# The reciprocal roots of a turn's layer norm and group norm taken in one chain of steps

## The chip, the cores and the metric

The kernel runs on one NeuronCore of a Trainium2 chip. The metric is the device time of one execution in microseconds (us). Engines are named as in the profile: PE is TensorE (PEld its weight loads), DVE is VectorE, ACT is ScalarE, POOL is GpSimd, SP is SyncE.

## The reference

Input x has 16 samples of 256 vertices (or channels), each with 16x16 values. Two residual blocks follow each other, each fed by a group norm of 32 groups:

```python
x = x + _L0_conv_ref(_gn(x), ...)     # graph convolution with temporal and spatial attention
x = x + _L1_conv_ref(_gn(x), ...)     # mixture of 8 experts, the best 2 for each token

# end of _L0_conv_ref
y = jax.nn.relu(res + tc)
mu = jnp.mean(y, axis=-1, keepdims=True)
var = jnp.var(y, axis=-1, keepdims=True)
return (y - mu) / jnp.sqrt(var + 1e-05) * gamma + beta

def _gn(v, G=32, eps=1e-05):
    g = v.reshape(B_, G, C_ // G, H_, W_)
    m = jnp.mean(g, axis=(2, 3, 4), keepdims=True)
    s = jnp.var(g, axis=(2, 3, 4), keepdims=True)
    return ((g - m) / jnp.sqrt(s + eps)).reshape(v.shape)
```

The change is about the two places with `1 / sqrt(...)` in the middle of the kernel: the layer norm that ends the first block, and the group norm that begins the second.

## The kernel before, in words

The kernel has four stages: the temporal attention for groups of four samples, then the middle stage with one sample per turn (spatial attention, graph convolution, temporal convolution, layer norm, group norm, routing), then the 72 tiles of the experts, then the sum of both experts' rows with the residual.

The change lies in the middle stage. It is a software pipeline of 21 turns, i from -2 to 18. A turn works on six samples at once, each in another phase: `ahead2` is sample i+2 (product of the spatial attention), `ahead1` i+1 (softmax, features), `now` i (graph and temporal convolution), `back1` i-1 (layer norm), `back2` i-2 (group norm, tokens), `back3` i-3 (routing). Turns -2 to 3 and 14 to 18 are written out, turns 4 to 13 are five passes of a loop with two turns each. Every engine has its own `turn` that issues its share in a fixed order; an engine never overtakes, and semaphores `b_...` hold it until another engine's result is there.

On DVE some of the work is cut into generators. `weave(a, b, ...)` takes one step of each in rotation until all are through; `along=` names generators that get a step in each round, but are not waited for. So a chain of small steps, each waiting for the one before, is mixed with other work. DVE's turn is: `centre` (L1167 to L1173), `router(route_a)` with `statistics`, then `attention` (L1133 row maximum, L1136, then L1142, the reciprocal of the sums) along with the norm's generator and `choice` (`route_b`, the choice of experts, L1253 to L1274), then the rest of the norms with `matrices` (L1151 twice, L1126) and `choice`, and last `route_c` (L1282 to L1289, the slots of the tokens).

The steps that count below:

- `ln_b` (L1182) sums the squares, `ln_roots` takes 32 reciprocal roots, `ln_c` (L1202) scales the layer norm's values and lets POOL go on with `ln_out`: L892, L893, L895, three operations over 128x512 values. POOL's result is needed by DVE's `gn_stats` (L1207) in the next turn.
- `gn_moments` (L1219 to L1222) waits for PE's `gn_mean` (L516) by `b_g1`; PE's `gn_var` (L520) then gives `b_g2`; `gn_roots` takes two reciprocal roots and `gn_scale` (L1228, L1229) gives `b_nb`. That is what ACT's `normalise` (L769, then PE's tokens, L528) and PE's `prefix` (L549 to L553) wait for. DVE's L1282 waits for `prefix` by `b_pf`.
- L1142 waits for ACT's exponentials (L736). ACT's `scale` (L745) waits for L1142, and PE's `turn_softmax` (L474) for ACT.
- PE's order in a turn is logits L463, graph L492, mix L448, `gn_mean` L516, graph L492, `turn_softmax` L474, `gn_var` L520, graph L492, features L483, product L455, convolution L504 and L509, features L483, `prefix` L549 to L553, tokens L528 and L533, L541.

`reciprocal_root` is a guess from the bits and three Newton steps, with the first line 13 operations of DVE, each waiting for the one before:

Of the kernel before, what the change touches and what calls it, by code (L numbers as in the profile page):

```python
# [66 lines left out]
def done(b):  # L67

    return b + (1 + START)
# [48 lines left out]
def build(nc, x, consts, small, cheb, vst, bst, w13t, w2t, xrows, yrows, out):  # L118
    with ExitStack() as ctx:
# [3 lines left out]
        def sem(name):  # L123
            return ctx.enter_context(nc.semaphore(name))
# [123 lines left out]
        v_ln = sem("v_ln"); v_gn = sem("v_gn"); v_rt = sem("v_rt"); v_rt2 = sem("v_rt2"); v_rt3 = sem("v_rt3"); v_lq = sem("v_lq"); v_gq = sem("v_gq")  # L248
# [703 lines left out]
        def _(dve):  # L952
# [233 lines left out]
            def ln_roots(b, p):  # L1186
                dve.wait_ge(s["b_var"], done(b))
                step = Steps(dve, v_lq, b, 13)
                yield from step.then(V.tensor_scalar(vq[:, 0, LN], vq[:, 4, LN], 1.0 / T, EPS, ALU.mult, ALU.add))
                yield from reciprocal_root(step, vq[:, :, LN], vr[:, LN])  # L1190
                step.close()

            def gn_roots(b, p):
                dve.wait_ge(s["b_g2"], done(b))
                step = Steps(dve, v_gq, b, 13)
                yield from step.then(V.tensor_scalar(vq[:, 0, GN], bank[2][:, 0:C], EPS, None, ALU.add))
                yield from reciprocal_root(step, vq[:, :, GN], vr[:, GN])
                step.close()

            def ln_c(b, p):  # L1200
                yv = yvs[p]
                V.tensor_tensor(yv, yv, th(vr[:, LN]), ALU.mult).then_inc(s["b_dn"], 1)  # L1202
                yield
# [90 lines left out]
            def turn(i, q, ahead2, ahead1, now, back1, back2, back3):  # L1294
# [21 lines left out]
                def layer_norm():  # L1316
                    if back1:
                        yield from ln_b(i - 1, 1 - q)
                        yield from ln_roots(i - 1, 1 - q)
                        yield from ln_c(i - 1, 1 - q)  # L1320

                def group_norm():
                    if back2:
                        yield from gn_moments(i - 2, q, step)
                        yield from pause(2)
                        yield from gn_roots(i - 2, q)
                        yield from gn_scale(i - 2, q)
# [17 lines left out]
                variance = layer_norm()  # L1345
                weave(attention(), along=(variance, choice))
                weave(variance, group_norm(), matrices(), choice)
# [172 lines left out]
```

## Time and profile before

| | |
|---|---|
| median of 3 runs | 752.15 us (751.39 to 752.87) |
| span of the profiled execution | 748.2 us; its own time with what lies around the span is not listed |
| middle stage | from about 110 us to 430 us of the span |
| PE busy | 587.2 us (78%) |
| DVE busy | 429.4 us (57%), 1895 instructions |
| ACT, POOL busy | 251.6 us, 208.3 us |

The shares are means over four stages with different limits. In the loop of the middle stage (187 to 393 us of the span) PE and DVE are both busy for some nine tenths of the time, so that neither share alone says which one sets a turn's length. In the timeline the columns are start in us, duration in us, engine, line, operation, result <- operands, shapes, and xN where N neighbouring instructions are merged. A bracket at the end is the idle time of the engine just before, and what ended it.

### The profile page before, as it was taken

How to read it: one execution, taken by the hardware profiler on the slowest of the kernel's cores; microseconds unless marked ns; L12 is line 12 of the kernel's file. 1: busy time of each engine (PE TensorE's matmuls, PEld its weight loads, DVE VectorE, ACT ScalarE, POOL GpSimd, SP SyncE). 2: the span in 40 equal slices, each digit the busy share in tenths (PEclk: the TensorE clock that was granted, in tenths of full speed). 3: DMA queues.
4: the chain of work that ended last, by engine and by line, in shares of the span. 5: the costliest groups of instructions: out<-in, count | busy, mean ns of one | idle time of the engine just before them, and what ended most of it. 6: DMA issues, size and time to landing. Idle time of an engine off the chain costs nothing. (4 is left out here: it accounts for less than half of the span.)

```text
span 748.2 us, 13145 instructions
## 1 busy us (share of the span) xinstructions
PE 587.2 (78%) x2520; PEld 372.1 (50%) x2521; DVE 429.4 (57%) x1895; ACT 251.6 (34%) x626; POOL 208.3 (28%) x267
## 2 busy tenths in 40 slices
PE   0556669999999999999983328999999999999343
PEld 0333337766666666666661114555555555555222
DVE  6666423778989888888888633232332333232255
ACT  0312224454545444444422102232232322232232
POOL 1000000114333333333455321333333333333100
PEclk9866659999999999999995559999999999999655
DMA  8900000000000000000000141222222222221496
GB/s 262 401 8 0 0 1 1 0 1 30 30 29 28 28 28 28 28 28 28 28 30 29 57 107 57 71 78 71 77 73 80 70 77 76 75 80 54 136 306 231
DMA packets 36439, 52.82 MB, mean 71 GB/s; under 512 B 4669, under 2 KB 31552, under 8 KB 36160
## 3 DMA queue, kind: packets, MB, share of 16 engines
q1 hardware_dynamic: 24960, 30.99, 13.2%
q0 software_dynamic: 6528, 16.86, 6.5%
q10 hardware_dynamic: 4928, 4.72, 1.9%
q8 instruction: 8, 0.13, 0.1%
q14 instruction: 15, 0.12, 0.1%
HBM read 30.32 MB, written 23.27 MB: 72 GB/s over the span
## 5 line engine op out<-in xcount | busy, mean ns | idle before, releaser
L612 PE MATMUL bank<-w,xT 128*128 x288 | 139.2, 606 | 14.9 <-DVE xT L1406 12.4
L1395 DVE COPY xT<-bank 128x256 f32<-128x256 f32 x72 | 30.6, 425 | 165.6 <-PE bank L600 163.6
L935 POOL DMA_INDIRECT yrows<-xT,dest x72 | 70.4, 978 | 169.4 <-ACT xT L821 163.1
L492 PE MATMUL bank<-work 128*128 128x256 f32 x384 | 94.5, 389 | 0.0
L904 POOL DMA_INDIRECT xrows<-xtok,slot x64 | 64.1, 1001 | 82.2 <-DVEq L1292 67.5
L892 POOL TENSOR_TENSOR yg<-work,sml 128x512 f32<-128x512 f32 x16 | 18.0, 1125 | 223.7 <-DVE work L1202 223.7
L627 PE MATMUL bank<-w,xT 128*128 x288 | 76.4, 388 | 1.3 <-ACT xT L826 1.3
L612 PEld LDWEIGHTS bank<-w,xT 128*128 128x128 f32 x288 | 49.5, 192 | 54.8 <-issue 54.8
L492 PEld LDWEIGHTS bank<-work 128*128 128x128 f32 x384 | 71.3, 193 | 9.3 <-issue 0.8
L815 ACT ACTIVATE xT<-bank 128x256 f32<-128x256 f32 x72 | 27.7, 385 | 113.8 <-PE bank L612 113.8
L627 PEld LDWEIGHTS bank<-w,xT 128*128 128x128 f32 x288 | 49.0, 190 | 9.4 <-issue 5.7
L821 ACT COPY xT<-bank 128x256 f32 (+1 forms) x72 | 26.8, 372 | 71.1 <-PE bank L627 70.1
L600 PEld LDWEIGHTS bank<-cst,xT 128*128 128x128 f32 x144 | 17.7, 143 | 62.9 <-SPq L316 31.7
L483 PE MATMUL bank<-thetabd,xTb 128*128 128x384 f32 x128 | 46.6, 487 | 0.0
L600 PE MATMUL bank<-cst,xT 128*128 128x128 f32 x144 | 29.9, 290 | 15.3 <-SPq L316 15.3
L663 PE MATMUL bank<-cst,xT 128*128 128x128 f32 x64 | 17.8, 433 | 30.6 <-DVE xT L1428 30.6
L769 ACT ACTIVATE xn<-xs,gr 128x256 f32 (+1 forms) x32 | 17.5, 593 | 71.2 <-DVE gr L1229 71.2
L463 PE MATMUL bank<-sg,vs 128*128 128x256 f32 x128 | 33.4, 406 | 2.5 <-ACT sg L731 1.4
L1151 DVE TENSOR_TENSOR work<-bank,chebs 128x768 f32<-128x768 f32 x32 | 30.0, 946 | 5.1 <-PE bank L474 5.1
L1406 DVE TENSOR_TENSOR xT<-bank,xT 128x256 f32<-128x256 f32 x72 | 30.6, 425 | 2.0 <-ACT xT L815 2.0
L751 ACT COPY work<-bank 128x384 f32<-128x384 f32 x64 | 28.9, 473 | 7.2 <-PE bank L483 6.5
L528 PE MATMUL bank<-xn,sml 128*8 128x256 f32 x64 | 19.0, 426 | 14.4 <-ACT xn L769 14.4
(205 smaller groups left out, 1061.0 us busy)
## 6 DMA issues: line engine op xcount, KB each, us to landing
xT<-xrows SPq DMA_DIRECT2D x72, 129.0 KB
xT<-yrows SPq DMA_DIRECT2D x32, 256.0 KB, 4.0
xs<-x_in SPq DMA_DIRECT2D x4, 1024.0 KB, 6.4
w<-w13t_in SPq DMA_DIRECT2D x1, 4096.0 KB, 15.2
out<-xT ACTq DMA_DIRECT2D x16, 256.0 KB, 3.8
w<-w2t_in SPq DMA_DIRECT2D x1, 2048.0 KB, 19.4
yrows<-xT,dest POOLq DMA_INDIRECT x72, 2.4
xrows<-xtok,slot POOLq DMA_INDIRECT x64
```

The source lines that it names most:

```text
L463: last = mm(bank[1][:, c * N:(c + 1) * N], vs[:, j, c * P:(c + 1) * P], sg[:, p, j], start=(j == 0), stop=(j == C - 1))
L483: mm(bank[4 + h][:, 0:K * P], xTb[:, p, h, c * P:(c + 1) * P], thetabd[:].rearrange("p k t o -> p (k t o)"), start=True, stop=True).then_i ...
L492: last = mm(bank[6][:, h * N:(h + 1) * N], z[:, p, c, k, h], A[:, p, c, k], start=(c == 0 and k == 0), stop=(c == C - 1 and k == K - 1))
L600: last = nc.tensor.transpose(bank[q][:, c * P:(c + 1) * P], xt[:, q, c * P:(c + 1) * P], ident)
L612: last = mm(bank[2 + q][:, :], xc[:, q, c], w13[:, e, c].rearrange("p w n -> p (w n)"), start=(c == 0), stop=(c == C - 1))
L627: last = mm(bank[4 + q][:, 0:N], hT[:, q, f], w2[:, e, f], start=(f == 0), stop=(f == C - 1))
L751: nc.scalar.copy(z[:, p, c, :, h], bank[4 + h][:, 0:K * P].rearrange("p (k o) -> p k o", k=K)).then_inc(s["b_zc"], 1)
L904: pool.indirect_dma_start(xrows, bass.IndirectOffsetOnAxis(ap=slot[:, q, w, k:k + 1], axis=0), xtok[:, q, k], None).then_inc(sc_done[q], 16)
L935: pool.indirect_dma_start(yrows, bass.IndirectOffsetOnAxis(ap=dest[:, q], axis=0), yo[:, q], None, bounds_check=2 * TOKENS - 1, oob_is_err ...
L1151: ins = V.tensor_tensor(A[:, p, c], p3, chebs[:, c], ALU.mult)
L1395: V.tensor_copy(xc[:, q].rearrange("p c k -> p (c k)"), bank[q][:, 0:C * P]).then_inc(c_xc, 1)
L1406: V.tensor_tensor(hh[:, q].rearrange("p f k -> p (f k)"), bank[2 + q][:, C * P:2 * C * P], gl[:, q].rearrange("p f k -> p (f k)"), ALU.mul ...
```

## The change

`ln_roots` and `gn_roots` become one `roots`, which fills columns 0 to 31 of `vq` from the layer norm and columns 32 and 33 from the group norm and then takes one chain over 34 columns. It needs `b_var` and `b_g2` at its start. The generators `layer_norm` and `group_norm` become one `norms`, in the order `ln_b`, `gn_moments`, two pauses, `roots`, `ln_c`, `gn_scale`.

```diff
-            def ln_roots(b, p):
-                dve.wait_ge(s["b_var"], done(b))
-                step = Steps(dve, v_lq, b, 13)
-                yield from step.then(V.tensor_scalar(vq[:, 0, LN], vq[:, 4, LN], 1.0 / T, EPS, ALU.mult, ALU.add))
-                yield from reciprocal_root(step, vq[:, :, LN], vr[:, LN])
-                step.close()
-
-            def gn_roots(b, p):
-                dve.wait_ge(s["b_g2"], done(b))
-                step = Steps(dve, v_gq, b, 13)
-                yield from step.then(V.tensor_scalar(vq[:, 0, GN], bank[2][:, 0:C], EPS, None, ALU.add))
-                yield from reciprocal_root(step, vq[:, :, GN], vr[:, GN])
+            def roots(turn, of_ln, of_gn):
+
+                if of_ln:
+                    dve.wait_ge(s["b_var"], done(turn))
+                    ins = V.tensor_scalar(vq[:, 0, LN], vq[:, 4, LN], 1.0 / T, EPS, ALU.mult, ALU.add)
+                if of_gn:
+                    dve.wait_ge(s["b_g2"], done(turn - 1))
+                    ins = V.tensor_scalar(vq[:, 0, GN], bank[2][:, 0:C], EPS, None, ALU.add)
+                both = slice(0 if of_ln else C * 16, NV if of_gn else C * 16)
+                step = Steps(dve, v_rq, turn, 13)
+                yield from step.then(ins)
+                yield from reciprocal_root(step, vq[:, :, both], vr[:, both])
                 step.close()
...
-                def layer_norm():
+                def norms():
+
                     if back1:
                         yield from ln_b(i - 1, 1 - q)
-                        yield from ln_roots(i - 1, 1 - q)
-                        yield from ln_c(i - 1, 1 - q)
-
-                def group_norm():
                     if back2:
                         yield from gn_moments(i - 2, q, step)
                         yield from pause(2)
-                        yield from gn_roots(i - 2, q)
+                    if back1 or back2:
+                        yield from roots(i - 1, back1, back2)
+                    if back1:
+                        yield from ln_c(i - 1, 1 - q)
+                    if back2:
                         yield from gn_scale(i - 2, q)
...
-                variance = layer_norm()
-                weave(attention(), along=(variance, choice))
-                weave(variance, group_norm(), matrices(), choice)
+                both = norms()
+                weave(attention(), along=(both, choice))
+                weave(both, matrices(), choice)
```

The wait for both norms' inputs stands in new lines: L1189 before is L1190 now, L1196 is L1193. The other lines named here keep their numbers. PE, ACT, POOL and SP issue what they issued before, in the same order.

The first place is on DVE in turn 3 (every later turn up to 14 has the same order), from the last step of the row maximum, L1136, to the reciprocal L1142 of the softmax. Before:

```order
L1136 TENSOR_SCALAR nmx<-nmx 128x2 [waits v_mx]
L1189 TENSOR_SCALAR vq<-vq 128x32 [waits b_var]
L1254 RECIPROCAL r<-r 128x2 [waits v_rt2]
L992 TENSOR_SCALAR vq<-vq 128x32 [waits v_lq]
L1255 TENSOR_TENSOR rt<-rt,r 128x16 [waits v_rt2]
L993 TENSOR_SCALAR vr<-vq 128x32 [waits v_lq]
L1258 TENSOR_REDUCE r<-rt 128x2 [waits v_rt2]
L1142 RECIPROCAL es<-es 128x2 [waits b_exp]
```

The same place in the changed kernel, up to the first step that waits for `b_g2`:

```order
L1136 TENSOR_SCALAR nmx<-nmx 128x2 [waits v_mx]
L1219 COPY gd<-bank 128x2 [waits b_st,b_g1]
L1220 TENSOR_TENSOR gd<-mv,bank 128x2
L1254 RECIPROCAL r<-r 128x2 [waits v_rt2]
L1221 TENSOR_TENSOR gd<-gd 128x2 [waits v_gn]
L1255 TENSOR_TENSOR rt<-rt,r 128x16 [waits v_rt2]
L1222 TENSOR_TENSOR gd<-gd,mv 128x2 [waits v_gn]
L1258 TENSOR_REDUCE r<-rt 128x2 [waits v_rt2]
L1142 RECIPROCAL es<-es 128x2 [waits b_exp]
L1259 TENSOR_TENSOR rt<-rt,r 128x16 [waits v_rt2]
L1260 TENSOR_TENSOR rt<-rt,cst 128x16 [waits v_rt2]
L1193 TENSOR_SCALAR vq<-bank 128x2 [waits b_g2]
```

The group norm's moments moved ahead of L1142, the layer norm's first steps moved behind it, and nothing but two steps of `route_b` and L1190 (left to DVE between L1260 and L1193) stands between L1142 and the wait for `b_g2`.

The second place is the end of the same turn on DVE, from the last L1151 to the first steps of `route_c`. L1202 stands there now; before, it stood right ahead of the two rows L995 and L1267, some 20 rows earlier:

```order
L1151 TENSOR_TENSOR work<-bank,chebs 128x768
L1273 TENSOR_TENSOR wts<-r 128x2 [waits v_rt2]
L1274 TENSOR_TENSOR wts<-r 128x2
L1001 TENSOR_TENSOR vr<-vr,vq 128x34 [waits v_rq]
L1126 TENSOR_TENSOR sg<-bank,bs 128x512 [waits b_L,b_pr]
L1202 TENSOR_TENSOR work<-work,vr 128x512 [waits v_rq,v_rt2]
L1228 COPY gr<-vr 128x2 [waits b_xn]
L1229 SCALAR_TENSOR_TENSOR gr<-gd,vr 128x2
L1282 TENSOR_TENSOR rt<-bank,cnt 128x16 [waits b_pf]
L1283 TENSOR_TENSOR cnt<-cnt,bank 128x8 [waits v_rt3]
L1284 TENSOR_TENSOR rt<-rt,cst 128x16
L1285 TENSOR_TENSOR rt<-rt 128x16 [waits v_rt3]
```

Here before:

```order
L1151 TENSOR_TENSOR work<-bank,chebs 128x768
L1273 TENSOR_TENSOR wts<-r 128x2 [waits v_rt2]
L1274 TENSOR_TENSOR wts<-r 128x2
L996 SCALAR_TENSOR_TENSOR vq<-vq,vr 128x2 [waits v_gq]
L1126 TENSOR_TENSOR sg<-bank,bs 128x512 [waits b_L,b_pr]
L1003 SCALAR_TENSOR_TENSOR vr<-vq,vr 128x2 [waits v_gq,v_rt2]
L995 TENSOR_TENSOR vq<-vq,vr 128x2 [waits v_gq]
L996 SCALAR_TENSOR_TENSOR vq<-vq,vr 128x2 [waits v_gq]
L999 SCALAR_TENSOR_TENSOR vq<-vq,vr 128x2 [waits v_gq]
L1001 TENSOR_TENSOR vr<-vr,vq 128x2 [waits v_gq]
L1228 COPY gr<-vr 128x2 [waits b_xn,v_gq]
L1229 SCALAR_TENSOR_TENSOR gr<-gd,vr 128x2
```

The last five steps of the group norm's own chain are gone from behind L1126, and L1202, which lets POOL begin, came to stand between L1126 and L1228.

## Rows read from the trace of the kernel before

**Rows 1.** The head of the page.

```profile
span 748.2 us, 13145 instructions
```

**Rows 2.** Timeline of DVE: L1136 in turns 4 and 13, L1121 after a loop pass.

```profile
185.41 0.32 DVE L1136 TENSOR_SCALAR nmx<-nmx 128x2 f32<-128x2 f32 x1
...
216.72 0.21 DVE L1121 COPY ghb<-gh 128x96 f32 x1 [0.77 <-DVE slot L1289]
...
350.48 0.16 DVE L1136 TENSOR_SCALAR nmx<-nmx 128x2 f32<-128x2 f32 x1
```

**Rows 3.** Timeline of one turn of the loop, DVE and PE, to the next L1136.

```profile
222.33 0.16 DVE L1136 TENSOR_SCALAR nmx<-nmx 128x2 f32<-128x2 f32 x1
...
223.57 0.17 DVE L1142 RECIPROCAL es<-es 128x2 f32<-128x2 f32 x1 [0.47 <-ACT pe_ L736]
...
224.88 0.60 PE L474 MATMUL bank<-cst,pn 128*128 128x128 f32 x4
...
225.70 0.15 DVE L1196 TENSOR_SCALAR vq<-bank 128x2 f32<-128x2 f32 x1
...
226.52 0.69 DVE L1202 TENSOR_TENSOR work<-work,vr 128x512 f32<-128x512 f32 x1
...
229.58 0.94 DVE L1151 TENSOR_TENSOR work<-bank,chebs 128x768 f32<-128x768 f32 x1
...
231.19 0.68 DVE L1126 TENSOR_TENSOR sg<-bank,bs 128x512 f32<-128x512 f32 x1
231.26 1.45 PE L483 MATMUL bank<-thetabd,xTb 128*128 128x384 f32 x4
...
232.83 0.15 DVE L1229 SCALAR_TENSOR_TENSOR gr<-gd,vr 128x2 f32<-128x2 f32 x1
...
233.04 0.18 PE L549 MATMUL bank<-mb,tri 128*128 128x8 bf16 x1 [0.32 <-DVE gr L1229]
...
233.35 0.18 DVE L1282 TENSOR_TENSOR rt<-bank,cnt 128x16 f32<-128x16 f32 x1 [0.37 <-PE bank L553]
...
233.65 0.17 DVE L1284 TENSOR_TENSOR rt<-rt,cst 128x16 f32<-128x16 f32 x1
...
234.26 1.03 PE L528 MATMUL bank<-xn,sml 128*8 128x256 f32 x4 [0.95 <-ACT xn L769]
234.42 0.17 DVE L1289 CAST slot<-slotf 128x4 int32<-128x4 f32 x1
...
234.85 0.21 DVE L1121 COPY ghb<-gh 128x96 f32 x1 [0.26 <-DVE slot L1289]
...
240.28 0.16 DVE L1136 TENSOR_SCALAR nmx<-nmx 128x2 f32<-128x2 f32 x1
```

**Rows 4.** The same turn: POOL's three operations and DVE beside them.

```profile
227.30 1.12 POOL L892 TENSOR_TENSOR yg<-work,sml 128x512 f32<-128x512 f32 x1 [5.66 <-DVE work L1202]
227.32 1.12 DVE L996 SCALAR_TENSOR_TENSOR vq<-vq,vr 128x2 f32<-128x2 f32 x1
...
228.50 1.14 POOL L893 TENSOR_TENSOR yg<-yg,sml 128x512 f32<-128x512 f32 x1
...
229.83 1.27 POOL L895 TENSOR_TENSOR xs<-xs,yg 128x512 f32 x1 [0.19 <-POOL yg L893]
230.45 0.67 DVE L1273 TENSOR_TENSOR wts<-r 128x2 f32 x1
```

**Rows 5.** Timeline of PE in turn 3.

```profile
168.35 0.38 PE L516 MATMUL bank<-mv,cst 128*128 128x2 f32 x2
...
169.97 0.60 PE L474 MATMUL bank<-cst,pn 128*128 128x128 f32 x4
```

**Rows 6.** Timeline of DVE at the end of turns 15 and 16.

```profile
392.80 1.07 DVE L1228 COPY gr<-vr 128x2 f32<-128x2 f32 x1
...
401.84 0.16 DVE L1196 TENSOR_SCALAR vq<-bank 128x2 f32<-128x2 f32 x1
...
408.16 0.15 DVE L1229 SCALAR_TENSOR_TENSOR gr<-gd,vr 128x2 f32<-128x2 f32 x1
```

More of the change, by code:

```diff
@@ L247, in build @@
         s = {n: sem(n) for n in names}
-        v_ln = sem("v_ln"); v_gn = sem("v_gn"); v_rt = sem("v_rt"); v_rt2 = sem("v_rt2"); v_rt3 = sem("v_rt3"); v_lq = sem("v_lq"); v_gq = sem("v_gq")
+        v_ln = sem("v_ln"); v_gn = sem("v_gn"); v_rt = sem("v_rt"); v_rt2 = sem("v_rt2"); v_rt3 = sem("v_rt3"); v_rq = sem("v_rq")
         p_x1 = sem("p_x1"); v_mx = sem("v_mx")
```

## The prediction

> **What bounds the kernel now.** The page gives the profiled span, 748.2 us [rows 1]; the runs' median is 752.15, so 3.95 us lie around the span, and I carry a difference of spans over to the median. I then read the timeline of DVE for the length of a turn: L1136 comes at 185.41 in turn 4 and at 350.48 in turn 13, 165.07 us for nine turns, 18.34 each [rows 2]. The turn from 222.33 to 240.28 is one of the short ones, 17.95 [rows 3]; every second one is longer by the loop's branch (0.77 us idle ahead of L1121 in place of 0.26, and 5.61 in place of 5.43 from L1121 to L1136) [rows 2, 3].
>
> Which engine sets these lengths is read from the waits. PE stands still twice at a turn's end, 0.32 us ahead of L549 for DVE's L1229, and 0.95 ahead of L528 for ACT, which itself waited for L1229 [rows 3]. DVE in the same turn waits 0.47 us for ACT's exponentials and 0.37 for L549 to L553, and otherwise issues one step after the other. So DVE bounds the turn, and PE has about 1.3 us to spare. Part of DVE's time is not its own: L996, over two columns, took 1.12 us and ended with POOL's L892, which had started 0.02 us earlier; L1273 took 0.67 and ended with POOL's L895. L1229, also over two columns and with two operands from SBUF, takes 0.15 [rows 3]. In the tail a two-column copy, L1228, took 1.07 the same way [rows 4, 6]. What these three have in common is data read from SBUF on both engines.
>
> **The change, step by step.** I lay out a loop turn anew, with time 0 at the start of PE's L474 (224.88 in rows 3).
>
> Removed: 12 small instructions per full turn. While several generators take turns, one costs about 0.1 us (the eight rows from L1196 to L1202 take 0.82) [rows 3]; the last five of the group norm's chain are alone and wait for each other, 0.2 each, from L1126's end at 231.87 to L1228 just ahead of L1229. With the 1.0 us that L996 lost to POOL and the 0.5 of L1273, some 3.2 us of DVE's turn go. Two columns more per step are nothing beside that: L1202 takes 0.69 us for 512 columns [rows 3], which makes 0.003 for two.
>
> Moved, first: L1219 goes ahead of L1142, and waits for L516. In the loop PE is early there once DVE is later, see below, so L1142 still comes 1.24 after L1136, set by the exponentials. L474 follows 1.31 behind L1142 [rows 3]. No change here.
>
> Moved, second: the whole chain waits for `b_g2`. L520 stands behind L474 on PE, and L1196, which waited for it, came 0.82 after L474 began, so 2.13 after L1142 [rows 3]. That time was filled with layer norm steps before. Now DVE has L1259, L1260 and L1190, 0.3 us, and then stands still for about 1.7 us. L1193 is at 0.8. Behind it are all of `route_b`, both L1151, L1126, L1202 and L1229.
>
> From L1193: 20 rows in rotation up to the first L1151, 2.3 us; both L1151 with two rows between, 1.87; L1273, L1274, L1001, 0.2; L1126, 0.6; so L1202 is at 0.8 + 5.0 = 5.8, and L1229, 0.7 later, at 6.5. Before it was at 232.83 - 224.88 = 7.95. The chain's saving is thus 1.45 us, the stall already paid.
>
> Now the rest of the turn. PE ends the second L483 at 232.71, 7.83 after L474, and nothing before that depends on the moved steps, so `prefix` can't start sooner. L1282 comes 0.31 after L549's start: 8.15 where it was 8.47. Of the 1.45 us, 0.3 are left: **PE's own order takes the rest**, and DVE waits about 1.1 us for `b_pf`.
>
> Moved, third: L1202 from 1.64 to 5.8. POOL's L892 starts 0.78 behind it, at 6.55 (L1228 and L1229 are issued just ahead and slip by); L893 runs from 7.75 to 8.9, L895 from 9.1 to 10.35 [rows 4]. Before, all three were over at 6.2, ahead of `route_c`; now they lie upon it. L1284 reads two SBUF operands at 8.45 and is held to 8.9. L1285 and L1286 are issued 0.05 and 0.15 later, in the 0.19 us between L893 and L895. L1289, a cast from SBUF to SBUF, would start at 9.5 and is held to 10.38 if it behaves as the copy in rows 6 did. L1121 comes 0.26 behind, at 10.64. Before it was at 9.97. From there to the next L1136 and L474 nothing changes.
>
> So a short turn grows by 0.67, to 18.6. For a long one the same sum gives 10.38 + 0.77 + 5.61 + 2.55 = 19.3. Their mean is 18.95 against 18.34: **+0.6 us a turn, for ten turns +6**.
>
> The rule weighed against these rows: the Trainium skill, "SBUF — State Buffer", section "Who interferes with whom", says that `copy`, `cast` and `tensor_scalar` can all take the port pair that VectorE shares with GpSimd, that a VectorE instruction with two SBUF inputs contends with a GpSimd instruction that reads SBUF, and that the one issued first keeps the other out altogether. Rows 4 and 6 agree for two inputs and for a copy; no row shows a cast beside POOL. By the rule L1289 is held and the sum is +6 for the loop; by a reading of the rows that leaves casts free, it is the second rival below.
>
> Turns outside the loop. In turn 3 PE is the later one: L516 ends at 168.73, L1219 is held until then, L1142 comes seven small rows later at 169.4, and L474 at 170.7 where it was 169.97 [rows 5]. Turn 2, with no `route_c`, comes out within 0.3 of before by the same sum. With the held rows of `route_c`, which in unrolled turns meet a shorter gap on POOL (below), turn 3 costs +2. In turns 14 to 16 PE has less to do, there is no attention, and DVE's chain is bare. From L1196 to L1229 in turn 16 takes 6.32 us, with L996's kind of hold twice and a held copy [rows 6]. One chain of 12 steps at 0.22, L1202 and L1228 make 3.4: -2.9. Turn 15 has the same structure, but POOL's work falls on its `route_c`; I keep -1.0 for turns 14 and 15 together. Sum: +6 + 2 - 3.9 = **+4**. Time 752.15 + 4 = 756.
>
> **Unknown costs, from both sides.** A cast beside POOL: at least 0.17, its time alone [rows 3], at most until L895 ends, 0.9; I take the latter. L1286 against L895: free if issued in the gap, otherwise held until L895 ends, which puts L1289 behind it and costs 0.5 more a turn; I take free in the loop, held in the unrolled turns. The wait of L1219 in the loop: L516 ended at 223.64, 1.3 behind L1136; as L1121 now comes 0.67 later against the same PE order, and more against PE's own pace, between 0 and 0.3; I take 0, and up to 0.5 is hidden behind the exponentials.
>
> **The rivals.**
>
> A, *faster*: POOL doesn't hold up `route_c`, because L892 to L895 meet only instructions that are issued ahead of them. Then L1289 is at 9.2, L1121 at 9.65, a turn costs -0.3 to -0.4, the loop -4; with turn 3 at +0.6 and the tail's -4.5 that is -8, so 744. For it: rows 4 show instructions that slip by. Against it: L1284 and L1289 fall well inside L893 and L895. L895 ends 4.55 behind L1202's start and L1289 is due 3.7 behind it, so it decides when L1202 comes 0.9 earlier against L1282 than I have it, or when POOL is that much quicker.
>
> B, *no change*: the cast isn't held. Only L1121, a copy, is, until 10.4. A turn is then within 0.1 of what it was, turn 3 costs +1.5, the tail gives -3.9: -2, so 750. For it: nothing in the rows shows a cast held. Against it: the copy.
>
> C, *slower still*: L1286 is held in the loop as well. +1.1 a turn, +11 for the loop, +9 in all: 761. The margin is 0.05 us, so it is open.
>
> D, the group norm's result being earlier shortens the turn as a whole, since L549 and L528 stop waiting. PE's idle 1.3 us would go, ten times, 13 us with the tail 739 or less. Against it: L474 then waits for L1142 instead, and the loop L474, `b_g2`, chain, `b_pf`, L1136, L1142, L474 is closed over both engines. It would need L1142 not to move with `route_c`.
>
> **How the numbers follow.** My forecast has 0.48, C 0.17, B 0.15, A 0.12, D 0.03, and 0.05 for slower yet. A measurement of this kernel tells about 0.2%, 1.5 us, from no change. Slower holds mine, C and the rest, less the low edge of mine: 0.64. B is split between faster and same; with the low edge of mine, same has 0.15 and faster 0.21. The range goes from 748.5, between B and A, to 762, the upper side of C. My forecast's own range is 753 to 759.
>
> **What would show it.** After the change L1142 stands as before 1.25 behind L1136. L1193 shows a wait of 1.5 us or more for L520 in the loop. PE's L549 no longer waits for L1229, L474 waits for ACT by 1 us or so instead. L1282 waits about 1 us for L553. L996 and L1273 have lost their long cases; L1284 and L1289 take 0.5 and 1 us. L1136 repeats at 18.9 us. The tail from L1193 to L1229 in turn 16 takes 3.4 us. I am wrong if L1289 shows 0.17 throughout, if L1286 shows over 1 us in the loop, or if L1219 waits so long that L1142 comes later than 1.3 behind L1136.

## The result and the profile after

The changed kernel took 762.12 us, median of 4 runs (760.19 to 763.9), against 751.77 (750.63 to 752.87) for the kernel before: 10.35 us more, ratio 1.0141 with a 95% interval of 1.0109 to 1.0173. The forecast was 756.0 with a range of 748.5 to 762.0. The sign was right, the size was not: the median lies just above the range.

The head and the first two rows of the page after:

```profile
span 760.5 us, 12883 instructions
...
PE 592.6 (78%) x2520; PEld 374.7 (49%) x2521; DVE 412.6 (54%) x1715; ACT 252.0 (33%) x626; POOL 208.2 (27%) x267
```

DVE is 17 us less busy than the 429.4 of before and has 180 instructions fewer, and the kernel is slower. What was removed is gone; the time went into waits.

One short turn of the loop after, DVE, PE and POOL, in the columns of [rows 3]. Time 0 of the prediction is 272.07:

```profile
269.58 0.16 DVE L1136 TENSOR_SCALAR nmx<-nmx 128x2 f32<-128x2 f32 x1
...
270.83 0.17 DVE L1142 RECIPROCAL es<-es 128x2 f32<-128x2 f32 x1 [0.43 <-ACT pe_ L736]
...
272.07 0.66 PE L474 MATMUL bank<-cst,pn 128*128 128x128 f32 x4 [1.92 <-ACT pn L745]
...
272.88 0.16 DVE L1193 TENSOR_SCALAR vq<-bank 128x2 f32<-128x2 f32 x1 [1.48 <-PE bank L520]
...
278.13 0.68 DVE L1202 TENSOR_TENSOR work<-work,vr 128x512 f32<-128x512 f32 x1
...
278.80 0.16 DVE L1229 SCALAR_TENSOR_TENSOR gr<-gd,vr 128x2 f32<-128x2 f32 x1
278.90 1.12 POOL L892 TENSOR_TENSOR yg<-work,sml 128x512 f32<-128x512 f32 x1 [9.99 <-DVE work L1202]
...
280.10 0.17 DVE L1282 TENSOR_TENSOR rt<-bank,cnt 128x16 f32<-128x16 f32 x1 [1.14 <-PE bank L553]
280.10 1.12 POOL L893 TENSOR_TENSOR yg<-yg,sml 128x512 f32<-128x512 f32 x1
...
280.38 0.87 DVE L1284 TENSOR_TENSOR rt<-rt,cst 128x16 f32<-128x16 f32 x1
...
281.38 0.17 DVE L1286 TENSOR_TENSOR rt<-rt 128x16 f32<-128x16 f32 x1
281.41 1.27 POOL L895 TENSOR_TENSOR xs<-xs,yg 128x512 f32 x1 [0.19 <-POOL yg L893]
...
281.86 0.85 DVE L1289 CAST slot<-slotf 128x4 int32<-128x4 f32 x1
283.08 0.21 DVE L1121 COPY ghb<-gh 128x96 f32 x1 [0.37 <-DVE slot L1289]
...
288.45 0.16 DVE L1136 TENSOR_SCALAR nmx<-nmx 128x2 f32<-128x2 f32 x1
```

The reader is to see three things. L1202, which stood 1.64 behind L474 [rows 3], now stands 6.06 behind it, and POOL's three operations with it. L1284 takes 0.87 and ends with L893; L1289 takes 0.85 and ends with L895, where both took 0.17 before. L1286, issued 0.03 us ahead of L895, takes 0.17. And L1229, 6.73 behind L474 where it was at 7.95, hardly helps: L1282 comes 8.03 behind L474 after a wait of 1.14, where it was at 8.47, and L1121 11.01 behind it, where it was at 9.97.

The windows of the same trace, one row for each stretch (its bounds and length, busy time and count of PE, PEld, DVE, ACT and POOL, then the granted clock of TensorE, whose 1.00 is the level of 2.4 GHz and whose 0.5 is that of 1.2, then the share and the GB/s of the DMA engines):

```profile
229.94:250.18 20.24, 18.32 (x87) 12.86 (x86) 14.71 (x72) 8.75 (x21) 7.40 (x7) 0.92 0.06 23
...
234.00:238.00 4.00, 4.00 (x10) 2.38 (x9) 3.95 (x23) 1.46 (x3) 0.00 (x0) 0.62 0.00 0
...
189.87:385.41 195.54, 174.88 (x867) 125.05 (x866) 149.26 (x691) 86.91 (x210) 74.36 (x71) 0.97 0.08 27
```

The short turn above took 18.87. The one from 229.94 took 20.24, and over four of its microseconds the mean clock was 0.62, so TensorE was at the lower level for most of them. Over the same ten turns the kernel before had 183.16 us and a clock of 1.00. What PE did ahead of the fall:

```profile
232.42 0.66 PE L474 MATMUL bank<-cst,pn 128*128 128x128 f32 x4 [1.92 <-ACT pn L745]
...
233.05 2.33 PE L492 MATMUL bank<-work 128*128 128x256 f32 x6
...
235.18 2.40 PE L483 MATMUL bank<-thetabd,xTb 128*128 128x384 f32 x4
```

It stood still for 1.92 us. Then six matmuls of L492 took 2.33 us, where they take 1.54 in other turns, and four of L483 2.40 instead of 1.45. Such turns are three of ten, 20.63, 20.24 and 20.22 us long; the other two short ones are 18.87 and 18.89, the long ones 19.39 to 19.44 (the last, with no branch behind it, 19.07). In the three turns PE is late with `prefix` (L1282 comes 9.7 behind L474 after a wait of 2.04), and L1285, two operands from SBUF, is the step that is held by L895 (1.24 in this one); L1284 and L1289 take 0.17.

The accounts of the two profiled executions (760.5 - 748.2 = +12.3):

| part of the span | before | after | difference |
|---|---|---|---|
| to the first L1136 (no changed instruction) | 109.92 | 112.55 | +2.6 |
| turns -1 to 2 | 56.23 | 55.89 | -0.3 |
| turn 3 | 19.26 | 21.43 | +2.2 |
| ten turns of the loop | 183.16 | 195.54 | +12.4 |
| turn 14 to the last L1289 | 61.12 | 58.21 | -2.9 |
| after it | 318.51 | 316.88 | -1.6 |

The first and the last row hold no changed instruction. The first stage of the other kernels, which is the same code, took 110.0 to 112.1 in their profiles, so its +2.6 is mostly scatter. The changed stage alone accounts for +11.3.

The tail, turn 16, beside [rows 6]:

```profile
418.20 0.16 DVE L1193 TENSOR_SCALAR vq<-bank 128x2 f32<-128x2 f32 x1
...
422.00 0.15 DVE L1229 SCALAR_TENSOR_TENSOR gr<-gd,vr 128x2 f32<-128x2 f32 x1
...
423.37 1.10 DVE L1286 TENSOR_TENSOR rt<-rt 128x16 f32<-128x16 f32 x1
...
424.79 1.02 DVE L1289 CAST slot<-slotf 128x4 int32<-128x4 f32 x1
```

From L1193 to L1229 it is 3.80 us, where it was 6.32 from L1196 on. Here both L1286 and L1289 are held.

### The profile page after: what moved, and what is told of

It reads as the page before. It is cut to its first block, busy times and chain, and to the rows that moved or that the text cites. A ratio compares the mean times of both kernels' runs of the same rounds, so it can differ in the third digit from the quotient of the medians.

```text
span 760.5 us, 12883 instructions
## 1 busy us (share of the span) xinstructions
PE 592.6 (78%) x2520; PEld 374.7 (49%) x2521; DVE 412.6 (54%) x1715; ACT 252.0 (33%) x626; POOL 208.2 (27%) x267
## 4 chain that ended last, share of the span: by engine, by line
PE 52%; DVE 21%; issue 12%; DMA 6%; ACT 5%; POOL 1%; SPq 1%; DVEq 1%; POOLq 0%; ACTq 0%
PE bank L612 14%; PE bank L627 7%; PE bank L483 6%; PE bank L492 5%; DMA xT<-yrows 4%; PE bank L382 3%; PE bank L455 2%; PE bank L600 2%; PE bank L504 2%; PE bank L509 2%; DVE work L1167 2%; PE bank L463 1%; PE bank L474 1%; ACT pe_ L736 1%; DVE work L1173 1%
## 5 line engine op out<-in xcount | busy, mean ns | idle before, releaser
L492 PE MATMUL bank<-work 128*128 128x256 f32 x384 | 96.3, 395 | 0.0
L892 POOL TENSOR_TENSOR yg<-work,sml 128x512 f32<-128x512 f32 x16 | 18.0, 1125 | 281.7 <-DVE work L1202 281.7
L492 PEld LDWEIGHTS bank<-work 128*128 128x128 f32 x384 | 72.0, 195 | 9.6 <-issue 0.8
L483 PE MATMUL bank<-thetabd,xTb 128*128 128x384 f32 x128 | 48.4, 502 | 0.0
L769 ACT ACTIVATE xn<-xs,gr 128x256 f32 (+1 forms) x32 | 17.5, 593 | 48.9 <-DVE gr L1229 48.9
L1151 DVE TENSOR_TENSOR work<-bank,chebs 128x768 f32<-128x768 f32 x32 | 30.2, 953 | 5.1 <-PE bank L474 5.1
L483 PEld LDWEIGHTS bank<-thetabd,xTb 128*128 128x128 f32 x128 | 24.5, 200 | 10.6 <-issue 1.5
```

The source lines that it names most:

```text
L483: mm(bank[4 + h][:, 0:K * P], xTb[:, p, h, c * P:(c + 1) * P], thetabd[:].rearrange("p k t o -> p (k t o)"), start=True, stop=True).then_i ...
L492: last = mm(bank[6][:, h * N:(h + 1) * N], z[:, p, c, k, h], A[:, p, c, k], start=(c == 0 and k == 0), stop=(c == C - 1 and k == K - 1))
L1151: ins = V.tensor_tensor(A[:, p, c], p3, chebs[:, c], ALU.mult)
```

## The experiments

All were timed beside the kernel before, which had a median of 750.41 beside experiments 1 to 4, 750.28 beside 5 to 8, 749.76 beside 9 to 11 and 750.8 beside 12. Ratios are to that median, with a 95% interval; where a median is set against one of another comparison, a difference of 1 or 2 us says little. The questions came in this order: is it the place of POOL's work; what do the clock's falls cost; do the moved moments or PE's order cost anything; which arrangement would use what the merged chain gives.

**1. The kernel before with only L1202 moved behind the group norm's chain.**

```diff
                 def layer_norm():
                     if back1:
                         yield from ln_b(i - 1, 1 - q)
                         yield from ln_roots(i - 1, 1 - q)
-                        yield from ln_c(i - 1, 1 - q)
+                        if not back2:
+                            yield from ln_c(i - 1, 1 - q)
...
                         yield from gn_roots(i - 2, q)
+                        if back1:
+                            yield from ln_c(i - 1, 1 - q)
                         yield from gn_scale(i - 2, q)
```

> The kernel before with two separate chains, and one thing moved: where a turn has both norms, ln_c (L1202), which lets POOL begin, is issued after the group norm's chain, just ahead of gn_scale, as in the changed kernel. Theory P (place of POOL's work): the merged chain itself is worth next to nothing, since it ends where the group norm's own chain would end; what costs is that L892 to L895 now lie on route_c, hold L1284 and L1289, and that PE waits long for L745 ahead of L474. So this kernel is slower than before by 6 to 11 us, about as the changed one (10 us). Rival Q (the stall at b_g2 and the moments ahead of L1142 cost it): this kernel has neither, DVE does layer norm steps while it waits, so it is within 2 us of before.

763.77 us, ratio 1.0177 (1.0132 to 1.0223): as slow as the changed kernel, though two chains run as before and nothing waits for `b_g2` any earlier. Its timeline, of a long turn in which L474 began at 289.91, shows the same holds:

```profile
296.73 0.15 DVE L1229 SCALAR_TENSOR_TENSOR gr<-gd,vr 128x2 f32<-128x2 f32 x1
296.82 1.12 POOL L892 TENSOR_TENSOR yg<-work,sml 128x512 f32<-128x512 f32 x1 [9.34 <-DVE work L1202]
...
298.23 0.95 DVE L1284 TENSOR_TENSOR rt<-rt,cst 128x16 f32<-128x16 f32 x1
...
299.79 0.84 DVE L1289 CAST slot<-slotf 128x4 int32<-128x4 f32 x1
```

The place of L1202, and of POOL's work with it, is enough for the whole loss. The stall for `b_g2` isn't needed to explain any of it. PE's waits at L474 are 1.4 to 2.1 us here too, and three of the ten turns, at 20.6 to 20.7 us, have a fall of the clock.

The experiment also tells what the merged chain gives by itself. L1229 comes 6.82 behind L474 in this turn and 6.93 in a short one without a fall, against 6.73 in the changed kernel: nearly all of the 1.22 us by which it came earlier there are had with two chains, by moving L1202 alone.

**2. Two idle matmuls ahead of the wait for ACT on PE** (they write a bank that nobody needs then; line numbers rise by 2).

```diff
             def turn_softmax(b, p):
-                pe.wait_ge(s["b_pn"], done(b))
                 pe.wait_ge(s["b_A"], done(b - 1))
...
+                    for _ in range(2):
+                        mm(bank[3][:, 0:N], vs[:, 0, 0:P], bs[:, 0], start=True, stop=True)
+                pe.wait_ge(s["b_pn"], done(b))
                 for m in range(C):
```

> The changed kernel with two extra 128x256 matmuls per turn on PE (into bank 3, which the transposes overwrite right after) between the graph product and turn_softmax, in the time in which PE waits 1.4 to 1.9 us for L745. They add no result. Theory C (clock): in the profiled run of the changed kernel three loop turns ran 1.3 to 1.7 us longer with a granted clock of 0.92 in place of 1.00, behind PE's 1.9 us wait. With the gap filled every loop turn is at 1.00, all turns have 18.9 or 19.4 us, and the time is 3 to 5 us below the changed kernel's. Rival: the clock falls for another reason, or the long wait has no part in it; then the same number of turns shows 0.92 and the time is the same, or higher by up to 1 us a turn where PE had no room.

759.21 us, ratio 1.0111 (1.0068 to 1.0153), with more work in it than the changed kernel. PE's wait and the loop as a whole:

```profile
230.40 0.66 PE L476 MATMUL bank<-cst,pn 128*128 128x128 f32 x4 [1.06 <-ACT pn L747]
```

```profile
189.18:380.68 191.50, 178.78 (x907) 129.33 (x906) 149.81 (x690) 86.65 (x210) 74.41 (x71) 1.00 0.08 28
```

The clock stays at 1.00 through the loop, no turn is over 19.5, and the ten turns take 191.50 instead of 195.54. The falls of the clock cost the changed kernel 4 us of its profiled loop. The median is 2.9 us lower, 2.3 by the ratios; their intervals (1.0109 to 1.0173 for the changed kernel) overlap, so that the size rests on the profiled loops.

**3 and 4. POOL's work cut from three operations to one,** on the changed kernel and on the kernel before. Gamma and beta of the layer norm are not applied, so the output isn't the reference's; line numbers behind fall by 6 (L1276 is L1282, L1223 is L1229). The same edit in both:

```diff
-                step(nc.gpsimd.tensor_tensor(flat(yg[:]), flat(y[:, p]), over(sm("gamma")), ALU.mult))
-                step(nc.gpsimd.tensor_tensor(flat(yg[:]), flat(yg[:]), over(sm("beta")), ALU.add))
...
-                nc.gpsimd.tensor_tensor(xs[:, b], xs[:, b], yg[:], ALU.add).then_inc(s["b_x1"], 1)
+                nc.gpsimd.tensor_tensor(xs[:, b], xs[:, b], y[:, p], ALU.add).then_inc(s["b_x1"], 1)
```

> The changed kernel with gamma and beta of the layer norm left out: POOL adds y to x in one operation of 1.27 us and L892 and L893 are gone (the output is not the reference's). Theory P: POOL is through about 2.05 us behind L1202's start, L1284 comes 2.4 behind it or later, so nothing in route_c is held. L1289 and L1284 take 0.17, a short turn has about 17.7 us and a long one 18.2 to 18.4, PE waits less than 1 us at L474 and its clock stays at 1.00. The time is 16 to 20 us below the changed kernel's, and 2 to 6 below the same cut of the kernel before. Rival Q: the holds are a symptom; the stall at b_g2 stays, and this kernel is still 5 to 10 us slower than the same cut of the kernel before.

> The kernel before with the same cut: gamma and beta left out, one POOL operation in place of three. L996 is held for about 1.25 us in place of 1.1, L1273 is not held any more (0.5 us less). A turn is 0.3 to 0.5 us shorter, the time 4 to 7 us below before. Both theories agree on this one; it is the yardstick for the cut of the changed kernel.

740.24 us on the changed kernel (ratio 0.9866, 0.9822 to 0.991), 740.97 on the one before (0.9869, 0.9829 to 0.991). The cut is worth 22 us to the one and 9.4 to the other, more than was expected of either, and the 10 between them are gone. From the trace of the changed kernel with the cut, then of the other:

```profile
242.17 0.66 PE L474 MATMUL bank<-cst,pn 128*128 128x128 f32 x4 [0.45 <-ACT pn L745]
...
248.91 0.15 DVE L1223 SCALAR_TENSOR_TENSOR gr<-gd,vr 128x2 f32<-128x2 f32 x1
249.11 1.26 POOL L889 TENSOR_TENSOR xs<-xs,work 128x512 f32 x1 [9.73 <-DVE work L1196]
...
250.20 0.17 DVE L1276 TENSOR_TENSOR rt<-bank,cnt 128x16 f32<-128x16 f32 x1 [1.14 <-PE bank L553]
```

```profile
242.28 0.60 PE L474 MATMUL bank<-cst,pn 128*128 128x128 f32 x4
...
244.65 1.26 POOL L889 TENSOR_TENSOR xs<-xs,work 128x512 f32 x1 [5.31 <-DVE work L1196]
244.78 1.15 DVE L1263 TENSOR_SCALAR xtok<-r 128x2 f32<-128x2 f32 x1
...
249.71 0.15 DVE L1223 SCALAR_TENSOR_TENSOR gr<-gd,vr 128x2 f32<-128x2 f32 x1
...
250.25 0.17 DVE L1276 TENSOR_TENSOR rt<-bank,cnt 128x16 f32<-128x16 f32 x1 [0.40 <-PE bank L553]
```

L1223 comes 6.74 behind L474 in the one and 7.43 in the other, L1276 8.03 and 7.97. So the merged chain ends 0.7 us earlier, and this is worth nothing, because L1276 waits for PE. Even the 0.7 isn't the chain's own: in the second kernel L1263, over two columns, takes 1.15 and ends with POOL's L889, which begins 0.13 us ahead of it, and in the first nothing is held. The merge was expected to be worth 2 to 6 us here; the medians differ by 0.7, which isn't clear of noise.

**5. The moments put back behind L1142** (`pause(3)` ahead of `gn_moments` in the changed kernel).

> The changed kernel with gn_moments (L1219 to L1222) put back behind L1142, by three pauses ahead of it in turns that have attention. In the profile of the changed kernel L1219 waited for L516 only in turns 2 and 3 (1.94 and 2.43 us), and L1142 came 0.5 to 1.5 us late there; in the loop it didn't wait. Theory P: the moments' place is worth turns 2 and 3 alone, so this is 0 to 2.5 us below the changed kernel, and still over 6 us above the kernel before. Rival Q (the moments ahead of L1142 are what costs): 6 us or more below the changed kernel.

764.16 us, ratio 1.0183 (1.0155 to 1.0212). Turns without a fall of the clock are 18.9 and 19.4 as before the edit; four of ten, not three, are 20.3 to 20.9. One of the four is a long turn, with a wait of 1.76 at L474. The moved moments cost nothing in the loop. In turns 2 and 3, where L1219 waits for L516, their place does cost: with them back the two turns took 16.34 and 20.70 us instead of 16.71 and 21.43. The median doesn't show this 1.1 us: it was expected 0 to 2.5 below the changed kernel's and is 2 above, and the fourth fall alone, 1.5 us in the profile, goes against it.

**6. The changed kernel with PE's `prefix` ahead of the second features.**

```diff
-                if ahead1:
-                    features(i + 1, 1 - q, 1)
                 if back3:
                     prefix(i - 3, 1 - q)
+                if ahead1:
+                    features(i + 1, 1 - q, 1)
```

> The changed kernel with PE's prefix (L549 to L553) ahead of the second features (L483) in place of behind them. DVE's wait for b_pf, 1.13 us a turn in the changed kernel, should go. Theory P: POOL's L895 ends at the same time behind L1202 and holds L1289 up to there, so L1289 ends as before and a turn stays within 0.2 us; the time is within 3 us of the changed kernel's. Rival R (PE's order is what eats the gain, as the prediction put it): L1121 follows L1282 and comes about 1 us earlier, so 8 to 12 us below the changed kernel.

758.83 us, ratio 1.0094 (1.0063 to 1.0124).

```profile
268.18 0.66 PE L474 MATMUL bank<-cst,pn 128*128 128x128 f32 x4 [1.59 <-ACT pn L745]
...
275.43 0.18 DVE L1282 TENSOR_TENSOR rt<-bank,cnt 128x16 f32<-128x16 f32 x1 [0.37 <-PE bank L553]
...
276.29 1.10 DVE L1286 TENSOR_TENSOR rt<-rt 128x16 f32<-128x16 f32 x1
...
277.55 1.26 POOL L895 TENSOR_TENSOR xs<-xs,yg 128x512 f32 x1 [0.19 <-POOL yg L893]
277.71 1.13 DVE L1289 CAST slot<-slotf 128x4 int32<-128x4 f32 x1
279.21 0.21 DVE L1121 COPY ghb<-gh 128x96 f32 x1 [0.37 <-DVE slot L1289]
```

L1282 comes 7.25 behind L474, 0.78 earlier than in the changed kernel, and L1121 at 11.03, not earlier at all: L1286 is held by L893 and L1289 until L895 ends. The turns are 18.88 and 19.42, the first 19.33. What this kernel gains, 3.3 us by the medians (the intervals overlap), is the size of the falls: PE's wait is now 1.2 to 1.6 at L474 and a few tenths at L549, the clock is at 1.00 throughout the loop, and its ten turns take 191.7.

**7. An arrangement that puts POOL's work beside L1151 and L1126**, which read PSUM: the merged chain, moments behind L1142, `pause(10)` ahead of `weigh` made `pause(17)`.

```diff
                     if back2:
+                        if ahead1:
+                            yield from pause(3)
                         yield from gn_moments(i - 2, q, step)
...
-                        yield from pause(10)
+                        yield from pause(17)
                         yield from weigh(i + 1, 1 - q)
```

> The merged chain with DVE's order around it changed: moments behind L1142 (as in the run with the moments back), and both L1151 and L1126 behind gn_scale in place of inside the chain. POOL's three operations start about 1.7 us earlier against route_c and lie beside L1151 and L1126, which read PSUM and were never held. By theory P: L1202 at 3.5 us behind L474, POOL through at 8.2, just ahead of L1284 at 8.45; nothing is held, a short turn has 17.6 and a long one 18.3 us, PE's wait at L474 is under 1 us. The time is 6 to 11 us below the kernel before, 16 to 21 below the changed one. Rival Q: the stall at b_g2 was filled too, so it gains, but no more than 1.5 us a turn.

744.73 us, ratio 0.9905 (0.9874 to 0.9937), 17 us less than the changed kernel and 5.6 less than the kernel before, where 6 to 11 had been expected.

```profile
224.93 0.66 PE L474 MATMUL bank<-cst,pn 128*128 128x128 f32 x4 [1.10 <-ACT pn L745]
...
229.82 1.81 DVE L1151 TENSOR_TENSOR work<-bank,chebs 128x768 f32<-128x768 f32 x2
229.84 1.12 POOL L892 TENSOR_TENSOR yg<-work,sml 128x512 f32<-128x512 f32 x1 [8.12 <-DVE work L1202]
...
233.24 0.43 DVE L1284 TENSOR_TENSOR rt<-rt,cst 128x16 f32<-128x16 f32 x1
...
234.28 0.17 DVE L1289 CAST slot<-slotf 128x4 int32<-128x4 f32 x1
```

Two L1151 take 1.81 beside L892 and L893, no more than the 0.94 for each in rows 3. The cast is free; L1284 still meets the end of L895, for 0.26 us.

**8. The same with `prefix` ahead of the convolution as well**, and so of the second features too.

> The run before with PE's prefix moved ahead of the convolution, where b_nb and b_M are there already. L1282 comes at about 6.8 us behind L474, L1284 is held by L895 up to 8.2, L1289 is at 8.7 and L1121 at 9.1: 0.4 to 0.5 us a turn less than without this move, and then PE's own order (17.3 us) is as long as the turn. So 3 to 6 us below the run before. Rival: PE's waits for the prefix at the new place cost as much as DVE gets; then it is the same.

744.61 us, the same (ratio 0.991, 0.9877 to 0.9943), where 3 to 6 us less had been expected. L1282 comes 7.2 behind L474 instead of 8.0, and L1284 is then held 1.25 until L895 ends; L1121 is again 9.9 behind L474.

**9 and 10. Both ceilings lifted: POOL cut to one operation and `prefix` early**, on either kernel.

> The changed kernel with both ceilings lifted: PE's prefix ahead of the second features, and POOL's L892 and L893 left out (gamma and beta aren't applied, so the output isn't the reference's; one POOL addition is left). With POOL's cut alone the changed kernel took 740.24, short turns 17.5 and long 18.3, L1276 (L1282 before the cut) 8.03 behind L474 after a wait of 1.14 for L553. Theory (the chain gained time in itself, and PE's order was the next ceiling under POOL's): L1223 stays 6.7 behind L474, L1276 comes 0.5 behind it, at 7.2, the turn loses up to 0.8 until PE, busy 16.7 of a short turn, bounds it: short turns 16.8 to 17.1, some 5 us less than with POOL's cut alone, about 735. Rival (the merged chain gained nothing that the turn can use): the same as with POOL's cut alone, 740, since what follows L1276 waits for something else.

> The kernel before with the same two edits (gamma and beta aren't applied, so the output isn't the reference's; one POOL addition is left). With POOL's cut alone it took 740.97. Theory: its own two chains end at 7.43 behind L474 (L1223), so the early prefix brings L1276 forward only from 7.97 to 7.9: 0.1 a turn, 740. The difference between this run and the one on the changed kernel is what the merged chain is worth when nothing behind it is in the way: 5 us by the theory, 0 to 1 by the rival.

744.13 us on the changed kernel (ratio 0.9922, 0.9895 to 0.9949) and 747.31 on the one before (0.9965, 0.9947 to 0.9983). The merged kernel is 3.2 us faster here, the only pair in which it is; how much of it is the chain's own stays open, since L1263 is held in the other one here too (1.04). Both are slower than with the cut alone (740.24, 740.97), where the theory had 735 and 740. From the first:

```profile
241.93 0.16 DVE L1213 COPY gd<-bank 128x2 f32<-128x2 f32 x1 [1.31 <-PE bank L516]
...
250.69 0.18 PE L549 MATMUL bank<-mb,tri 128*128 128x8 bf16 x1 [0.35 <-DVE gr L1223]
...
251.30 0.69 DVE L1278 TENSOR_TENSOR rt<-rt,cst 128x16 f32<-128x16 f32 x1
```

L1276 did come forward, to 7.27, and so onto the one operation that POOL has left: L1278 is held by it for 0.5 us. And PE waits 0.35 for DVE at L549 with 1.54 us of features still to do behind it, and so comes late to L516, for which DVE then waits 1.31 us. The turns are 18.15 and 18.4 us, 0.36 more than with the cut alone, which is what PE waits at L549. That PE bounds the turn here is read from this agreement; no run takes the wait away by itself.

**11. The early `prefix` on the kernel before, alone.**

> The kernel before with PE's prefix ahead of the second features alone, nothing left out. L549 already waited 0.32 for L1229 there, so the edit can give only the time from L549's old place to L1229: L1229 at 7.95 behind L474, L1282 at 8.4 instead of 8.47, and L1289 isn't beside POOL. Theory: 0 to 0.1 a turn, 749 to 751. Rival: features moved behind it come too late for the next turn and it costs 0.3 a turn, 754.

752.24 us, ratio 1.0036 (1.0012 to 1.006): slower by 2.5 us, as the rival had it, though it had said 754. PE's L549 waits 1.46 to 1.61 us for L1229, which comes no earlier than before, and a turn is 0.3 to 0.4 us longer.

**12. The kernel before with `pause(8)` instead of `pause(10)` ahead of `weigh`**, nothing else: both L1151 stand a little sooner, beside L892 and L893.

> The kernel before, two chains as they were, with pause(10) ahead of weigh made pause(8): both L1151, which read PSUM, then stand three and one instructions ahead of where they stood, on the time of POOL's L892 and L893, in place of the two-column steps. It asks whether the merged chain is needed for the gain that the rearranged merged kernel had (744.73 against 750.28 of before), or whether putting PSUM work beside POOL does it alone. Theory (both are needed: the last five group norm steps stay alone, 0.2 each, and PE's order takes what is left): L996 loses most of its 1.12, L1273 or an L996 behind it still meets L895; L1229 from 7.95 to 7.2 to 7.6 behind L474; L1282 from 8.47 to 8.15 by PE's order, 0.3 a turn: 746.5 to 749. Rival (the place of L1151 is the whole gain): 744 to 746, the same as the rearranged merged kernel. Other rival (the hold only moves to other small steps): 750, no change.

743.97 us, ratio 0.9906 (0.9876 to 0.9937). The rival was right: the place of L1151 alone gives the gain.

```profile
227.89 0.95 DVE L1151 TENSOR_TENSOR work<-bank,chebs 128x768 f32<-128x768 f32 x1
227.98 1.13 POOL L892 TENSOR_TENSOR yg<-work,sml 128x512 f32<-128x512 f32 x1 [5.64 <-DVE work L1202]
...
229.07 0.15 DVE L996 SCALAR_TENSOR_TENSOR vq<-vq,vr 128x2 f32<-128x2 f32 x1
...
231.07 0.72 DVE L995 TENSOR_TENSOR vq<-vq,vr 128x2 f32<-128x2 f32 x1
```

L996 takes 0.15 where it took 1.12 [rows 4], L1273 0.15 where it took 0.67, and one L995 0.72, L1267 0.39 and L1269 0.33 in their place: the holds are shorter, not gone. The turns are 17.5 and 18.5, L1282 comes 8.07 behind L474. The merged chain gains nothing over this in the arrangement of experiment 7: ratio 0.9906 with two chains, 0.9905 with one.

## Why the prediction was right or wrong

**Removed work.** Right in the main: L1229 comes 1.22 us earlier after a wait of 1.48 for L520, where 1.45 and 1.7 were said. So 2.7 us a turn left DVE, not 3.2; the way from L1193 to the first L1151 is 22 rows and 2.50 us, not 20 rows and 2.3. In the 3.2 the prediction counted 1.5 us that L996 and L1273 lost to POOL. By experiment 1 these make nearly all of the 1.22: there both steps take 0.15 as well, L1202 alone was moved, and L1229 comes only 0.1 to 0.2 us later than with the merged chain. The 12 instructions saved and the stall for `b_g2` about cancel. The stall is not what costs.

**The moved moments.** Right in the loop (L1142 1.25 behind L1136, and experiment 5), and right in turn 3, where +2 was said and +2.2 came. The part of the moments there was to be 0.73 us (L474 at 170.7 instead of 169.97); putting them back shortened the turn by 0.73.

**"PE's own order takes the rest."** The wait of 1.1 us for `b_pf` came as said (1.14). As the cause it failed in the changed kernel: experiment 6 took most of the wait away and no turn without a fall became shorter, since POOL's L895 sets the end anyway. It is the next ceiling below: where POOL's work is cut (experiments 3 and 4) it makes 0.7 us in the chain worth nothing.

**POOL upon `route_c`.** The likeliest case, and right. L1284 is held (0.87, where 0.5 was said), the cast L1289 is held until L895 ends (0.85, where 1 was said), L1286 slips by. The last was a narrow thing: the prediction gave it a margin of 0.05 us and called it open, and it was issued 0.03 us ahead of L895. By the Trainium skill, "SBUF — State Buffer", section "Who interferes with whom", a cast can take the port pair shared with GpSimd and the one issued first keeps the other out; the traces agree, with 0.17 alone and 0.84 to 1.13 beside L895 in the loops of the changed kernel and of experiment 6. So rival B, a free cast, falls, and A with it. C, L1286 held in the loop, didn't occur there, though its 761 us is near to what was measured: that is chance, the time was made up otherwise. In turn 3 (1.25) and the tail (1.10) L1286 was held, as said. D falls: PE's wait moved to L474. Experiment 1 shows that the place alone makes the loss, and experiments 3, 4, 7 and 12 that it goes when POOL's work is shorter or lies beside instructions with one operand in PSUM.

**The size.** The stage came out at +11.3 where +4 was said. The term that was mis-sized is the loop, "+0.6 us a turn, for ten turns +6", which measured +12.4:

- 4.0 of the 6.4 that are missing are the falls of TensorE's clock in three turns. Two of them took 1.36 and 1.34 us more than the 18.88 of a short turn; the first, 20.63, is set against the 19.30 of the same turn in experiment 2, since the turn behind the unrolled ones is longer even without a fall. The ten turns of experiment 2 are 4.04 us shorter, which is the same. The step that failed is in rival D and in "what would show it": PE's idle time was said to move to L474 as "1 us or so", and no cost was put to it. It was 1.5 to 2.1 us at one place. The prediction's own terms gave that: PE's waits of 0.32 and 0.95 and the 0.67 by which a short turn grows make 1.94, and 1.92 was measured (0.18 was left at L528). The time that PE had to spare was taken for free, and it was not. Experiment 2, which only fills this wait, and experiment 6, which splits it, have no falls in the loop, and their ten turns are 4 us shorter.
- 2.4 are small terms: from L1193 to L1202 5.25 us, not 5.0, and from the end of L1289 to L1121 0.37, not 0.26. With 0.06 less in each of two other terms this gives the short turn of 18.87 where 18.6 was said, and the long one of 19.4 where 19.3 was. The first turn of the loop has 0.7 of the 2.4, 19.3 where 18.6 was said.

The tail gave -2.9, not -3.9. In turn 16 the interval from L1193 to L1229 is 3.80, not 3.4: from L1193 to L1202 (at 421.32) twelve steps took 3.12, 0.26 each where 0.22 was said. L1286 and L1289 are held behind it, by some 0.9 us each. Of the 7.3 us between +4 and +11.3 the clock has 4.0, the loop's small terms 2.4 and the tail 1.0; the other turns have -0.1.

What stays open: a wait of 1.92 us goes ahead of a fall at 232.42 and 348.61, and one of 1.92 or 1.93 of none at 272.07 and 310.33. What decides between them no row shows. In the loops of the changed kernel and of experiments 1 and 5 falls came after ten waits of 1.76 to 2.09 us at L474, and none after six others of 1.90 to 1.93. The kernels of experiments 2 and 6, in which no wait of PE at L474 in the loop is over 1.64 us, have none; that is all that is shown, from one profiled execution of each. And from before to after the median moved by 10.35, the stage by 11.3 in the profiled executions; no run separates the difference from scatter.

## What to carry to other kernels

Before an instruction is moved that lets POOL start, lay out what DVE does in the time in which POOL's work will then run: here small steps with two operands in SBUF, a copy, a cast and a `tensor_scalar` over two columns waited until POOL's operation ended (0.15 to 0.17 us alone, up to 1.25 beside it), and instructions with one operand in PSUM didn't (L1151 0.94, L1126 0.68), nor did reductions (L1287 0.17). Before two chains are merged, ask what the merged one waits for at its start, and what waits for its end; here 12 instructions a turn were saved, the stall for the later input took about as much, and at the end DVE waited for PE anyway. When one engine's idle time moves, add it up at its new place: here TensorE's waits of 0.32 and 0.95 us, made into one of some 1.9, were followed by a fall of its clock in three turns of ten, 1.3 to 1.4 us each.

## What the runs showed that was not expected

- **TensorE's clock.** With PE busy for nine tenths of the loop, the granted clock was 0.62 in the mean of four microseconds after a wait of 1.92 us at L474, and the turn took 1.4 us more. In the loops of these runs no wait of 1.74 us or less in that place was followed by a fall, and not every longer one was.
- **0.03 us decide.** L1286 was issued at 281.38 and L895 began at 281.41: the step took 0.17 us. In turn 16 L893 began at 423.29 and L1286 was issued at 423.37: 1.10 us.
- **An order that helps one engine's wait can cost the loop.** In the merged kernels the early `prefix` made L1282 come 0.8 us earlier, and L1121 no earlier with POOL's three operations there. With POOL's work cut it cost 3.9 us on the merged kernel and 6.3 on the one before (744.13 against 740.24, 747.31 against 740.97, in different comparisons), and 2.5 us on the kernel before alone; in the last two L1282 came no earlier, since it waits for L1229.
- **A change of one number beat the change of structure.** Two pauses fewer ahead of `weigh` gave 743.97, 18 us below the changed kernel and 6.8 below the kernel before in the same comparison.
